# State-space stage of a four-layer kernel: the softplus fix moved next to its subtraction, a wait added on GpSimd, and work re-ordered on TensorE and ScalarE

## The chip, the cores and the metric

The kernel runs on one core of a Trainium2 chip. The metric is the device time of one execution in microseconds; the runs of the kernel before give a median of 2456.47 us. Such a core has TensorE (PE) for matrix products, VectorE (DVE), ScalarE (ACT) and GpSimd (POOL) for elementwise work, and SyncE (SP), which here issues transfers. Each engine works its own list of instructions in order; between engines only semaphores order the work.

## What is computed

The model has four layers over an input of 2 x 2048 tokens of width 256. The change lies in the first, a state-space ("mamba") layer; the mixture of experts, the recurrent feed-forward layer, the attention and the last mixture are untouched. Cut to what matters:

```python
xm, z = jnp.split(x @ W_in.T, 2, axis=-1)               # 512 channels each
xc = silu(causal_conv4(xm) + conv_b)
dt, Bm, Cm = jnp.split(xc @ W_xproj.T, [R, R + N], axis=-1)   # R = 64, N = 16
delta = softplus(dt @ W_dt.T + b_dt)
dA  = exp(delta[..., None] * -exp(A_log))
dBx = delta[..., None] * Bm[:, :, None, :] * xc[..., None]
h = dA_t * h + dBx_t ;  y_t = einsum('ben,bn->be', h, C_t)    # scan over the tokens
out = ((y + D_skip * xc) * silu(z)) @ W_out.T
```

## The kernel before

The state-space stage (`mamba_phase`) works through 8 **units** of 512 tokens; the two batches alternate (`hf` is 0 or 1 in a loop of 4). A unit is 16 **states** n = 0 to 15, one for each component of the state vector, each over all 512 channels, which lie on the 128 partitions in four blocks c = 0 to 3. While a unit's 16 states run, the engines also prepare the next unit (`F`: projections, convolution, gates, dt, softplus) and finish the last one (gating, output projection, residual, norm). The order of all this is written out by hand, state by state.

In a state n each engine does this:

- **GpSimd** makes the products u * B of state n + 2 in two halves q (L399: one instruction of 1024 elements a partition, or in states 13 and 14 two of 512) and behind each half one addition: add (n, 1) and add (n, 3) sum ScalarE's weighted piece into the accumulator (L411). At n = 1 it also computes the scale of the row norm (L374, L376), at n = 13 the new u = delta * xc (L381, twice) and at n = 14 the RMS scale.
- **ScalarE** makes dA for state n + 1 in four pieces (`factor`, L559), weights the token blocks 1 and 3 of the transposed state n - 1 by C (`weighted`, L573; called part (n, 1) and part (n, 3) here, `a_part` in the trace), copies the carry, and does the tasks of `MID_ACT` and `END_ACT`. `END_ACT` stands between the third and the fourth piece of dA. At the end of state 8 that is `silus`: the SiLU of the gates z (L532, 2048 elements a partition) and of xc (L535, L498). `ACT_TABLE_LOAD` is a change of function table, to SiLU, back to exp, to ln, back.
- **VectorE** scans (L787, four pieces), weights and sums the token blocks 0 and 2 (L750), and takes softplus apart in four pairs of operations: `softplus_fix` (L691) and `softplus_sub` (L698) in state 12 and `softplus_add` (L705) in state 13. All of these read two tensors from SBUF, 1024 elements a partition.
- **TensorE** transposes h of state n - 1 in four **turns** j (L929), turns 0 and 1 ahead of the tasks in `EARLY`, turns 2 and 3 ahead of those in `LATE`. There are two PSUM tiles for the turns: turn (n, 1) waits until ScalarE has read part (n - 1, 3), turn (n, 3) until it has read part (n, 1), and turns 0 and 2 wait for VectorE's sums in the same way. Tasks are: f0 and f1 (transposes of the normed rows, which need ScalarE's `hn`), xc0 to xc3 (convolution, in four parts), dt (L871), d0 to d3 (delta), ct, z0 to z3, y0 to y3 (output of the last unit, L847 and L849), o0 and o1 (output projection, L882), g0, g1 and r.

GpSimd's products of state n + 2 wait for turn (n - 1, 3), since the buffer of h is used again, and add (n, j) waits for part (n, j). ScalarE's part (n, j) in turn waits for GpSimd's add (n - 1, j), since the part has one buffer for each j.

```python
EARLY = {2: ["f1"], 3: ["xc0.1"], 4: ["xc0.3"], ... 11: ["d2", "d3"], 12: ["o0"], 13: ["z0"], 14: ["z3"], 15: ["r"]}
LATE = {1: ["y0", "f0"], 2: ["y1", "xc0.0"], 3: ["y2", "xc0.2"], 4: ["y3"], ... 9: ["dt"], 10: ["d0", "d1"], ...}
weighted(U, n, 1, here); factor(U, n + 1, 0, there); ...   # ScalarE, state n
```

## Time and profile before

| | |
|---|---|
| runs, us | 2455.84, 2463.76, 2456.47; median 2456.47 |
| profiled execution | 2460.9 us, span 2459.2 us |
| granted TensorE clock, mean | 0.866 |
| busy over the span | PE 78%, DVE 68%, ACT 48%, POOL 62% |
| the eight units | from 80 to 1125 us of the span |

The profiled execution is 4.4 us above the median. Times below are microseconds from the start of its span. The state-space stage takes a little over two fifths of the span; the other layers follow it behind a barrier, so a microsecond won or lost in a unit is one in the total.

### The profile page before, as it was taken

What the parts mean: (1) busy time and instruction counts of PE and PEld (TensorE: products, weight loads), DVE (VectorE), ACT (ScalarE), POOL (GpSimd) and SP (SyncE); (2) the same over time, 40 slices, a digit from 0 to 9 for tenths busy, and PEclk for the clock granted to TensorE, in tenths of its full rate; (3) what the DMA queues carried; (4) which work ended last, traced back from release to release, by engine and by line L of the source; (5) the groups of instructions that cost most, each with busy time, mean ns of one, the idle gap of its engine ahead of it and who ended that gap; (6) DMA issues with size and microseconds to landing.
All of it is one profiled execution on the core that took longest, in us unless ns stands there. A gap on an engine that the chain in (4) does not pass through costs nothing. (4 is left out here: it accounts for less than half of the span.)

```text
span 2459.2 us, 35798 instructions
## 1 busy us (share of the span) xinstructions
PE 1911.8 (78%) x10252; PEld 1465.2 (60%) x10253; DVE 1678.1 (68%) x3193; ACT 1184.7 (48%) x2021; POOL 1515.8 (62%) x1152
## 2 busy tenths in 40 slices
PE   6787879686979787875599999907877784799970
PEld 2445455554555454544499999904655664699970
DVE  1779898989989898985644444437634897644438
ACT  2677777777777767773232222226632441111112
POOL 1799999999999999994133333335622420355532
PEclk9888979798989888887699999958988896799995
DMA  3111111111101011112411111142000014122226
GB/s 123 38 35 40 39 37 36 39 39 37 39 23 52 27 49 31 43 36 77 165 48 47 47 48 48 41 139 77 9 18 11 9 35 163 42 71 70 70 65 192
DMA packets 76780, 138.63 MB, mean 56 GB/s; under 512 B 10369, under 2 KB 47873, under 8 KB 75858
## 3 DMA queue, kind: packets, MB, share of 16 engines
q1 hardware_dynamic: 62994, 99.67, 12.4%
q0 software_dynamic: 13632, 37.24, 4.8%
q8 instruction: 56, 0.92, 0.2%
q14 instruction: 98, 0.80, 0.1%
HBM read 104.86 MB, written 32.01 MB: 56 GB/s over the span
## 5 line engine op out<-in xcount | busy, mean ns | idle before, releaser
L787 DVE TENSOR_TENSOR_SCAN a_hs<-a_dA,a_carry,a_hs 128x512 f32<-128x512 f32 x512 | 628.3, 1264 | 63.5 <-ACT a_dA L559 53.7
L399 POOL TENSOR_TENSOR a_hs<-a_u,a_b_bc 128x1024 f32<-128x1024 f32 (+1 forms) x292 | 634.9, 2182 | 2.3 <-POOL a_u L381 1.9
L929 PE MATMUL a_h_ps<-k_ident,a_hs 128*128 128x128 f32 x2064 | 328.3, 308 | 174.7 <-DVE a_acc L750 95.6
L929 PEld LDWEIGHTS a_h_ps<-k_ident,a_hs 128*128 128x128 f32 x2064 | 268.4, 158 | 293.5 <-DVE a_hs L787 86.2
L559 ACT ACTIVATE a_dA<-a_delta,a_a_neg 128x512 f32<-128x512 f32 x512 | 350.1, 687 | 39.6 <-DVE a_hs L787 38.4
L411 POOL TENSOR_TENSOR a_acc<-a_acc,a_part 128x512 f32<-128x512 f32 x242 | 331.7, 1371 | 28.6 <-ACT a_part L573 28.3
L573 ACT ACTIVATE a_part<-a_h_ps,a_c_tok 128x512 f32<-128x512 f32 x242 | 166.0, 686 | 203.8 <-PE a_h_ps L929 176.0
L1229 POOL DMA_INDIRECT expert_rows<-m0e_ys,k_pair x71 | 78.7, 1109 | 232.5 <-DVE m0e_ys L1285 221.6
L750 DVE SCALAR_TENSOR_TENSOR a_acc<-a_h_ps,a_c_tok,a_acc 128x512 f32<-128x512 f32 x242 | 176.3, 728 | 46.5 <-PE a_h_ps L929 46.4
L863 PE MATMUL a_fx<-a_hT,a_w_x 128*128 128x512 f32 x432 | 200.9, 597 | 2.2 <-ACT a_halo L495 1.4
L1295 DVE TENSOR_TENSOR m0e_hT<-m0e_gs,m0e_u 128x512 f32<-128x512 f32 x70 | 48.2, 688 | 191.5 <-ACT m0e_gs L1248 191.5
L1248 ACT ACTIVATE m0e_gs<-m0e_g 128x512 f32<-128x512 f32 x71 | 42.4, 597 | 270.0 <-PE m0e_u L1326 270.0
L1252 ACT ACTIVATE m1e_hT<-m1e_u 128x512 f32<-128x512 f32 x71 | 42.4, 597 | 226.3 <-PE m1e_u L1326 226.3
L1326 PE MATMUL m1e_u<-m1e_xT,m1e_wu 128*128 128x128 f32 x1136 | 140.1, 277 | 0.2 <-DVE m1e_wu L1279 0.2
L1326 PE MATMUL m0e_g<-m0e_xT,m0e_wg 128*128 128x128 f32 x1136 | 140.1, 277 | 0.0
L1326 PE MATMUL m0e_u<-m0e_xT,m0e_wu 128*128 128x128 f32 x1136 | 139.5, 276 | 0.0
L1275 DVE TENSOR_SCALAR m1e_xT<-m1e_x,k_ln_w,k_ln_b 128x128 f32<-128x128 f32 x142 | 51.7, 406 | 128.6 <-PE m1e_x L1314 128.6
L1229 POOL DMA_INDIRECT expert_rows<-m1e_ys,k_pair x71 | 70.2, 989 | 104.5 <-DVE m1e_ys L1285 90.1
L1336 PE MATMUL m0e_y<-m0w_down,m0e_hT 128*128 x568 | 134.5, 380 | 0.2 <-DVE m0e_ys L1285 0.2
L1326 PEld LDWEIGHTS m1e_u<-m1e_xT,m1e_wu 128*128 128x128 f32 x1136 | 134.1, 194 | 0.6 <-issue 0.6
L1326 PEld LDWEIGHTS m0e_g<-m0e_xT,m0e_wg 128*128 128x128 f32 x1136 | 134.2, 194 | 0.1
L1336 PE MATMUL m1e_y<-m1w_down,m1e_hT 128*128 x568 | 134.2, 379 | 0.0
(420 smaller groups left out, 3793.2 us busy)
## 6 DMA issues: line engine op xcount, KB each, us to landing
a_b_bc<-b_rows SPq DMA_DIRECT2D x132, 256.0 KB, 3.2
c_y<-expert_rows SPq DMA_DIRECT2D x16, 512.0 KB, 5.6
q_y<-expert_rows SPq DMA_DIRECT2D x16, 512.0 KB, 5.9
norm_rows<-a_x SPq DMA_DIRECT2D x9, 512.0 KB, 3.3
m0w_up<-in_m_up SPq DMA_DIRECT2D x1, 4096.0 KB, 12.1
m0w_gate<-in_m_gate SPq DMA_DIRECT2D x1, 4096.0 KB, 22.2
m0w_down<-in_m_down SPq DMA_DIRECT2D x1, 4096.0 KB, 32.1
c_xl<-in_L_attn_x SPq DMA_DIRECT2D x8, 512.0 KB, 3.7
```

Source lines behind the costliest of these rows:

```text
L399: last = pool.tensor_tensor(hs[k][:, w, :], u[s][:, w, :], b_bc[:, k:k + 1, :].broadcast_to([P, width, T]), ALU.mult)
L411: pool.tensor_tensor(acc[s][:, j, :], acc[s][:, j, :], part[:, j // 2, :], ALU.add).then_inc(s_add, 1)
L559: act.activation(dA[c][:], delta[s][:, c, :], ACT.Exp, scale=a_neg[:, c, k:k + 1]).then_inc(s_da, 1)
L573: act.activation(to, hT_ps[j % 2][:], ACT.Copy, scale=c_tok[s][:, j, k:k + 1]).then_inc(s_part, 1)
L750: dve.scalar_tensor_tensor(out=acc[s][:, j, :], in0=hT_ps[j % 2][:], scalar=weight, in1=acc[s][:, j, :], op0=ALU.mult, op1=ALU.add).then_i ...
L787: dve.tensor_tensor_scan(hs[k][:, c, :], dA[c][:], hs[k][:, c, :], carry[:, hf, c, n:n + 1], ALU.mult, ALU.add).then_inc(s_scan, 1)
L863: last = pe.matmul(ps[:], w_x[:, q, d, k * P:(k + 1) * P], hT[:, d, q:q + T], start=q == 0 and d == 0, stop=q == KC - 1 and d == DC - 1)
L929: last = pe.transpose(hT_ps[j % 2][:, c * P:(c + 1) * P], hs[(n - 1) % NBUF][:, c, j * P:(j + 1) * P], ident[:])
L1229: pool.indirect_dma_start(io["expert_rows"], bass.IndirectOffsetOnAxis(ap=per.pair[:, s:s + 1], axis=0), ys[s % 2][:], None).then_inc(s_st ...
L1275: last = dve.tensor_scalar(xT[k][:, c, :], x_ps[:, c, :], scale[:, c:c + 1], shift[:, c:c + 1], ALU.mult, ALU.add)
L1326: last = pe.matmul(ps[k][:, f, :], w[k][:, c, f * P:(f + 1) * P], xT[k][:, c, :], start=c == 0, stop=c == DC - 1)
L1336: last = pe.matmul(y_ps[k][:], hT[k][:, c, :], w_down[:, c, bass.ds(e * D, D)], start=c == 0, stop=c == FC - 1)
```

## The change

Seven edits, all in `mamba_phase`:

1. `softplus_fix` moves from the middle of state 12 to its end, directly ahead of `softplus_sub` (VectorE).
2. GpSimd, in state 13, waits for both pieces of the subtraction (`s_sub`) ahead of the products of state 15.
3. dt is split: its first two of four matmuls stay at the end of state 9, the other two come behind turn (10, 1) (TensorE).
4. f0 comes ahead of y0 at the end of state 1 (TensorE).
5. The SiLU of z leaves `silus` and becomes `gates`, in state 4 (ScalarE). It is the same z as before, that of the unit in progress, which VectorE multiplies in during the next unit.
6. `softplus_exp` moves behind the second piece of dA in state 11. Part (4, 3) then comes behind the third piece of dA of its state, part (11, 3) behind the fourth (`NEXT_ACT`).
7. In states 8, 10 and 11 (`LONG_END`) the fourth piece of dA comes ahead of the tasks at the end of the state.

```diff
--- before.py
+++ after.py
@@ -234,14 +234,16 @@
         s_p = m.sem("pool_chain")
 
         EARLY = {2: ["f1"], 3: ["xc0.1"], 4: ["xc0.3"], 5: ["xc1.0"], 6: ["xc1.3"], 7: ["xc2.2"], 8: ["xc3.1"],
-                 11: ["d2", "d3"], 12: ["o0"], 13: ["z0"], 14: ["z3"], 15: ["r"]}
-        LATE = {1: ["y0", "f0"], 2: ["y1", "xc0.0"], 3: ["y2", "xc0.2"], 4: ["y3"], 5: ["xc1.1", "xc1.2"], 6: ["xc2.0", "xc2.1"],
-                7: ["xc2.3", "xc3.0"], 8: ["xc3.2", "xc3.3"], 9: ["dt"], 10: ["d0", "d1"], 11: ["ct"], 12: ["o1"], 13: ["z1", "z2"],
+                 10: ["dt.2", "dt.3"], 11: ["d2", "d3"], 12: ["o0"], 13: ["z0"], 14: ["z3"], 15: ["r"]}
+        LATE = {1: ["f0", "y0"], 2: ["y1", "xc0.0"], 3: ["y2", "xc0.2"], 4: ["y3"], 5: ["xc1.1", "xc1.2"], 6: ["xc2.0", "xc2.1"],
+                7: ["xc2.3", "xc3.0"], 8: ["xc3.2", "xc3.3"], 9: ["dt.0", "dt.1"], 10: ["d0", "d1"], 11: ["ct"], 12: ["o1"], 13: ["z1", "z2"],
                 14: ["g0", "g1"]}
-        MID_ACT = {1: ["norms"], 2: ["f1"], 10: ["dt"], 11: ["d2", "d3", "exp"], 13: ["z0"], 14: ["x1", "z2", "z3"]}
+        MID_ACT = {1: ["norms"], 2: ["f1"], 10: ["dt"], 11: ["d2", "d3"], 13: ["z0"], 14: ["x1", "z2", "z3"]}
         END_ACT = {0: ["moments"], 1: ["f0"], 4: ["xc0"], 5: ["own"], 6: ["xc1"], 7: ["xc2"], 8: ["silus"], 10: ["d0", "d1"],
                    11: ["round", "ct"], 12: ["ln"], 13: ["z1"], 14: ["g0", "g1"], 15: ["rows"]}
         LEAD, SHORT = 2, (13, 14)
+        NEXT_ACT = {4: ["gates"], 11: ["exp"]}
+        LONG_END = (8, 10, 11)
         ON_X = ("f0", "f1", "xc0", "xc1", "xc3", "d0", "d2", "ct", "o1", "z1", "z3", "g1")
         FRONT = ["f0", "f1", "xc0", "xc1", "xc2", "xc3", "dt", "d0", "d1", "d2", "d3", "ct", "z0", "z1", "z2", "z3"]
 
@@ -437,6 +439,8 @@
                         pool.wait_ge(s_turn, lin(U, NS * TJ, TJ * (ahead - 2) + TURNED))
                         pool.wait_ge(s_carry, lin(U, NS, ahead - 2 + KEPT))
                         pool.wait_ge(s_bl[ahead % NBUF], loaded(U, ahead))
+                        if n == 13:
+                            pool.wait_ge(s_sub, lin(F, 2, 2))
                         for q in range(2):
                             product(U, ahead, q, hf if ahead < NS else 1 - hf)
                             add(U, n, 2 * q + 1, hf if n else 1 - hf)
@@ -526,10 +530,14 @@
                                           scale=R2[:, bass.ds(tile0 + j, 1)])
                 last.then_inc(s_rows, 1)
 
-            def silus(U, F, s):
+            def gates(U, s):
+
                 for name in ("z2", "z3"):
                     act.wait_ge(s_free[side(name)], count(name, before(U)))
-                act.activation(z[1 - s][:], z[1 - s][:], ACT.Silu).then_inc(s_zc, 1)
+                act.activation(z[s][:], z[s][:], ACT.Silu).then_inc(s_zc, 1)
+
+            def silus(U, F, s):
+
                 for c in range(EC - 1):
                     act.wait_ge(s_free[side(f"xc{c}")], count(f"xc{c}", U))
                     last = act.activation(xc[s][:, c, :], xc[s][:, c, :], ACT.Silu, bias=conv_b[:, c:c + 1])
@@ -624,6 +632,8 @@
                             layer_norms(i * TJ + BT * hf, hf)
                         elif name == "rows":
                             norm_rows(tile0)
+                        elif name == "gates":
+                            gates(U, hf)
                         elif name == "silus":
                             silus(U, F, 1 - hf)
                         else:
@@ -647,13 +657,21 @@
                         for name in MID_ACT.get(n, []):
                             task(name)
                         factor(U, n + 1, 1, there)
-                        weighted(U, n, 3, here)
+                        for name in NEXT_ACT.get(n, []):
+                            task(name)
+                        if n not in NEXT_ACT:
+                            weighted(U, n, 3, here)
                         if n == 15:
                             act.wait_ge(s_rr, lin(U, 1, 1))
                         factor(U, n + 1, 2, there)
+                        if n in LONG_END:
+                            factor(U, n + 1, 3, there)
+                        if n in NEXT_ACT:
+                            weighted(U, n, 3, here)
                         for name in END_ACT.get(n, []):
                             task(name)
-                        factor(U, n + 1, 3, there)
+                        if n not in LONG_END:
+                            factor(U, n + 1, 3, there)
             end = (0, 2 * NB, None)
             for j in OFF:
                 weighted(end, 0, j, 1)
@@ -802,8 +820,6 @@
                         if n == 14:
                             dve.wait_ge(s_free["X"], count("o1", U))
                             rms_stats(tile0, lin(U, 1, 1))
-                        if n == 12:
-                            softplus_fix(F, 1 - hf)
                         if n == 13:
                             softplus_add(F, 1 - hf)
                         scan(2)
@@ -811,6 +827,7 @@
                         summed(U, n, 2, here)
                         summed(U, n, 3, here)
                         if n == 12:
+                            softplus_fix(F, 1 - hf)
                             softplus_sub(F, 1 - hf)
                             dve.wait_ge(s_full["Y"], count("o0", U))
                             dve.wait_ge(s_xn, lin(U, 1, 1))
@@ -867,7 +884,7 @@
                         last = pe.matmul(ps[:], w_z[:, d, k * P:(k + 1) * P], hT[:, d, KC - 1:], start=d == 0, stop=d == DC - 1)
                 elif name == "dt":
                     pe.wait_ge(s_xc, lin(F, 1, 1))
-                    for c in range(EC):
+                    for c in range(EC) if part_ is None else (part_,):
                         last = pe.matmul(ps[0:R + 2 * NS, :], w_proj[:, c, :], xc[s][:, c, :], start=c == 0, stop=c == EC - 1)
                 elif name == "ct":
                     for j in range(TJ):
```

Three places, as the built programs list them. A name's last digit is the number of its buffer.

TensorE at the end of state 1, before: the turns of state 1 (L929, from hs0), y0 (L847, L849), f0 (L859), then the first turn of state 2 (from hs1).

```order
L929 MATMUL a_h_ps0<-k_ident,a_hs0 128x128 x4
L929 MATMUL a_h_ps1<-k_ident,a_hs0 128x128 x4
...
L847 MATMUL a_fy<-a_xc1,a_diag_d 128x512
L849 MATMUL a_fy<-k_ident,a_acc1 128x128 x4
...
L859 MATMUL a_fx<-k_ident,a_hn 128x128 x4
...
L929 MATMUL a_h_ps0<-k_ident,a_hs1 128x128 x4
L929 MATMUL a_h_ps1<-k_ident,a_hs1 128x128 x4
```

And now:

```order
L946 MATMUL a_h_ps0<-k_ident,a_hs0 128x128 x4
L946 MATMUL a_h_ps1<-k_ident,a_hs0 128x128 x4
...
L876 MATMUL a_fx<-k_ident,a_hn 128x128 x4
...
L864 MATMUL a_fy<-a_xc1,a_diag_d 128x512
L866 MATMUL a_fy<-k_ident,a_acc1 128x128 x4
...
L946 MATMUL a_h_ps0<-k_ident,a_hs1 128x128 x4
L946 MATMUL a_h_ps1<-k_ident,a_hs1 128x128 x4
```

f0, which reads `hn`, stands ahead of y0, and the turns of state 2 stand behind both as before.

ScalarE in state 4, before: part (4, 1) (L573), the pieces of dA for state 5 (L559), part (4, 3), the evacuation of xc0.

```order
L573 ACTIVATE a_part<-a_h_ps1,a_c_tok0 128x512
...
L559 ACTIVATE a_dA0<-a_delta0,a_a_neg 128x512
L645 ACTIVATE a_carry<-a_hs3 128x4
L559 ACTIVATE a_dA1<-a_delta0,a_a_neg 128x512
...
L573 ACTIVATE a_part<-a_h_ps1,a_c_tok0 128x512
...
L559 ACTIVATE a_dA2<-a_delta0,a_a_neg 128x512
...
L500 ACTIVATE a_xc1<-a_fx 128x512
L559 ACTIVATE a_dA3<-a_delta0,a_a_neg 128x512
```

And now:

```order
L581 ACTIVATE a_part<-a_h_ps1,a_c_tok0 128x512
...
L567 ACTIVATE a_dA0<-a_delta0,a_a_neg 128x512
L655 ACTIVATE a_carry<-a_hs3 128x4
L567 ACTIVATE a_dA1<-a_delta0,a_a_neg 128x512
...
L537 ACT_TABLE_LOAD
L537 ACTIVATE a_z0<-a_z0 128x2048
...
L567 ACT_TABLE_LOAD
L567 ACTIVATE a_dA2<-a_delta0,a_a_neg 128x512
...
L581 ACTIVATE a_part<-a_h_ps1,a_c_tok0 128x512
...
L504 ACTIVATE a_xc1<-a_fx 128x512
L567 ACTIVATE a_dA3<-a_delta0,a_a_neg 128x512
```

Between the second and the third piece of dA stand two changes of table and the SiLU of z, and part (4, 3) has moved behind the third piece.

VectorE in state 12, before: scans (L787, by piece of dA), sums (L750), the fix (L691), the subtraction (L698).

```order
L787 SCALAR_TENSOR_TENSOR a_hs0<-a_dA0,a_carry,a_hs0 128x512
L787 SCALAR_TENSOR_TENSOR a_hs0<-a_dA1,a_carry,a_hs0 128x512
...
L750 SCALAR_TENSOR_TENSOR a_acc0<-a_h_ps0,a_c_tok0,a_acc0 128x512
...
L691 SCALAR_TENSOR_TENSOR a_acc1<-a_acc1,a_u1 128x1024 x2
...
L787 SCALAR_TENSOR_TENSOR a_hs0<-a_dA2,a_carry,a_hs0 128x512
...
L787 SCALAR_TENSOR_TENSOR a_hs0<-a_dA3,a_carry,a_hs0 128x512
...
L750 SCALAR_TENSOR_TENSOR a_acc0<-a_h_ps0,a_c_tok0,a_acc0 128x512
...
L698 TENSOR_TENSOR a_delta1<-a_delta1,a_acc1 128x1024
```

And now:

```order
L805 SCALAR_TENSOR_TENSOR a_hs0<-a_dA0,a_carry,a_hs0 128x512
L805 SCALAR_TENSOR_TENSOR a_hs0<-a_dA1,a_carry,a_hs0 128x512
...
L768 SCALAR_TENSOR_TENSOR a_acc0<-a_h_ps0,a_c_tok0,a_acc0 128x512
...
L805 SCALAR_TENSOR_TENSOR a_hs0<-a_dA2,a_carry,a_hs0 128x512
...
L805 SCALAR_TENSOR_TENSOR a_hs0<-a_dA3,a_carry,a_hs0 128x512
...
L768 SCALAR_TENSOR_TENSOR a_acc0<-a_h_ps0,a_c_tok0,a_acc0 128x512
...
L709 SCALAR_TENSOR_TENSOR a_acc1<-a_acc1,a_u1 128x1024 x2
...
L716 TENSOR_TENSOR a_delta1<-a_delta1,a_acc1 128x1024
```

All four scans and both sums now stand ahead of the fix.

## Rows read from the trace of the kernel before

**Rows 1.** The page's DMA issues: line, count, size of one, us to landing.
```profile
a_b_bc<-b_rows SPq DMA_DIRECT2D x132, 256.0 KB, 3.2
```

**Rows 2.** Windows, one unit; busy us (instructions) of PE, PEld, DVE, ACT, POOL, then clock.
```profile
457.26:586.76 129.50, 103.77 (x461) 67.39 (x460) 116.36 (x129) 94.93 (x166) 125.71 (x76) 0.87 0.12 38
```

**Rows 3.** Waits of GpSimd in the state-space stage: us in total, times, longest.
```profile
POOL a_acc L411 <- ACT a_part L573: 28.3, 27, 1.7
```

**Rows 4.** Timeline of GpSimd, states 9 to 13: start, length, line; in brackets idle before.
```profile
545.56 1.27 POOL L411 TENSOR_TENSOR a_acc<-a_acc,a_part 128x512 f32<-128x512 f32 x1 [0.61 <-ACT a_part L573]
...
553.68 1.27 POOL L411 TENSOR_TENSOR a_acc<-a_acc,a_part 128x512 f32<-128x512 f32 x1 [1.00 <-ACT a_part L573]
...
562.14 2.50 POOL L399 TENSOR_TENSOR a_hs<-a_u,a_b_bc 128x512 f32<-128x512 f32 x2
...
566.13 1.27 POOL L411 TENSOR_TENSOR a_acc<-a_acc,a_part 128x512 f32<-128x512 f32 x1 [1.50 <-ACT a_part L573]
567.36 3.48 POOL L399 TENSOR_TENSOR a_hs<-a_u,a_b_bc 128x512 f32<-128x512 f32 x2
...
577.70 3.35 POOL L399 TENSOR_TENSOR a_hs<-a_u,a_b_bc 128x1024 f32<-128x1024 f32 x1
```

**Rows 5.** Timeline of VectorE, softplus operations of state 12.
```profile
568.42 3.50 DVE L691 SCALAR_TENSOR_TENSOR a_acc<-a_acc,a_u 128x1024 f32<-128x1024 f32 x2 [1.10 <-ACT a_acc L547]
...
574.86 3.97 DVE L698 TENSOR_TENSOR a_delta<-a_delta,a_acc 128x1024 f32<-128x1024 f32 x2
```

**Rows 6.** Timeline of VectorE, the same operation ahead of the loop.
```profile
68.54 2.36 DVE L691 SCALAR_TENSOR_TENSOR a_acc<-a_acc,a_u 128x1024 f32<-128x1024 f32 x2 [51.15 <-ACT a_acc L547]
```

**Rows 7.** Timeline of TensorE, states 1 and 2.
```profile
487.78 1.63 PE L847 MATMUL a_fy<-a_xc,a_diag_d 128*128 128x512 f32 x2
...
490.55 0.66 PE L859 MATMUL a_fx<-k_ident,a_hn 128*128 128x128 f32 x4 [0.24 <-ACT a_hn L472]
491.05 1.34 PE L929 MATMUL a_h_ps<-k_ident,a_hs 128*128 128x128 f32 x8
```

**Rows 8.** Timeline of GpSimd, the adds (2,1) and (4,3).
```profile
495.24 1.28 POOL L411 TENSOR_TENSOR a_acc<-a_acc,a_part 128x512 f32<-128x512 f32 x1
...
512.96 1.31 POOL L411 TENSOR_TENSOR a_acc<-a_acc,a_part 128x512 f32<-128x512 f32 x1
```

**Rows 9.** Timeline of ScalarE, state 4.
```profile
506.16 0.69 ACT L573 ACTIVATE a_part<-a_h_ps,a_c_tok 128x512 f32<-128x512 f32 x1 [2.46 <-PE a_h_ps L929]
...
508.75 0.69 ACT L573 ACTIVATE a_part<-a_h_ps,a_c_tok 128x512 f32<-128x512 f32 x1 [0.62 <-PE a_h_ps L929]
```

**Rows 10.** Timeline of TensorE, turns (5,0), (5,1) and (8,2), (8,3).
```profile
510.23 1.04 PE L929 MATMUL a_h_ps<-k_ident,a_hs 128*128 128x128 f32 x8
...
533.83 1.04 PE L929 MATMUL a_h_ps<-k_ident,a_hs 128*128 128x128 f32 x8
```

**Rows 11.** Timeline of ScalarE, states 8 to 11.
```profile
536.88 1.28 ACT L532 ACT_TABLE_LOAD   x1
538.18 1.92 ACT L532 ACTIVATE a_z<-a_z 128x2048 f32<-128x2048 f32 x1
540.00 1.93 ACT L535 ACTIVATE a_xc<-a_xc,a_conv_b 128x512 f32<-128x512 f32 x3
...
554.13 0.58 ACT L506 ACTIVATE a_dbc<-a_fy 96x512 f32<-96x512 f32 x1
...
565.27 0.70 ACT L573 ACTIVATE a_part<-a_h_ps,a_c_tok 128x512 f32<-128x512 f32 x1
```

**Rows 12.** Timeline of TensorE, states 9 to 12.
```profile
546.07 5.77 PE L871 MATMUL a_fy<-a_xc,a_w_proj 128*96 128x512 f32 x8
...
566.03 1.11 PE L929 MATMUL a_h_ps<-k_ident,a_hs 128*128 128x128 f32 x4 [3.14 <-ACT a_part L573]
566.94 5.59 PE L882 MATMUL a_fy<-a_w_out,a_z 128*128 128x256 f32 x16
```

**Rows 13.** Windows, columns as in rows 2, at the clock's fall.
```profile
564.00:566.00 2.00, 0.00 (x0) 0.00 (x0) 0.60 (x1) 2.00 (x4) 0.64 (x1) 0.52 0.04 15
```

## The prediction

> **What bounds the kernel now.** I read the page first: 2459.2 us of span, of which the eight units take 1045, and SyncE's loads of B, which take 3.2 us to land [rows 1]. The windows come next. In one unit, from the start of one u product to the next, 129.5 us, GpSimd is busy 125.7, VectorE 116.4, TensorE 103.8 and ScalarE 94.9 [rows 2]. GpSimd is the bound, so the third view is what it waits for: 28.3 us in the whole stage, all for ScalarE's parts [rows 3]. The timeline places them. In the unit shown, add (9, 1) waits 0.61 us, add (10, 1) 1.00 and add (11, 3) 1.50 [rows 4], 3.1 in all, just behind the states in which ScalarE has silus and softplus.
>
> GpSimd's busy time is also longer than its work. The two products of q = 0 in state 12 take 3.48 us [rows 4], against 2.50 of the pair at 562.14, and in the same moment VectorE runs the fix. The fix takes 3.50 us for two operations and the subtraction 3.97 [rows 5]; ahead of the loop, with GpSimd idle, the same pair takes 2.36 [rows 6]. So each of these VectorE operations holds GpSimd up by 0.98 us. GpSimd pays that six times a unit, four times for fix and subtraction.
>
> **The change, part by part.** I follow that unit by its own clock, first what becomes later, then what becomes earlier. What decides is when VectorE has finished the subtraction, X, because GpSimd now waits for it.
>
> *f0 ahead of y0.* Before, y0 ran from 487.78 and was over when f0 started at 490.55, and f0 had waited for `hn` (0.24 us, ScalarE) [rows 7]. y0 filled a gap. Now TensorE stands idle until `hn` comes, does f0, and then y0, while turn (2, 0) is queued behind. Y0's own time is 2.5 us at least (490.31 - 487.78, with the clock rising within it). At the slower clock throughout it is more: it streams as many columns as half of dt's eight passes, which took 5.77 us with a faster end [rows 12], so 2.9 and up to 3.4. I take 3.0, nearest to these. Turn (2, 1) then ends at 491.05 + 1.34 + 3.0 = 495.4, ScalarE's part at 496.1 (0.69 a part, 0.16 for the signal), add (2, 1) starts at 496.25 instead of 495.24 [rows 8]: GpSimd 1.0 late. TensorE stays 3.0 late, since it works without a gap in these states.
>
> *Gates in state 4.* Part (4, 1) was waiting for TensorE [rows 9], so it comes at 506.16 + 3.0 = 509.16. To part (4, 3) it was 2.59 us, 0.62 of it waiting, so 1.97. Now a table change, the SiLU of z and a change back come between: 1.28 + 1.82 + 1.28 and small gaps, 4.5 (the SiLU from 538.18 to 540.00, the change at 536.88 [rows 11]), and one piece of dA, 0.6. Part (4, 3) comes at 516.2 and is there for GpSimd at 517.1; add (4, 3) would want it at 512.96 + 1.0 [rows 8], so 3.1 us more. GpSimd is now 4.1 late. Turn (5, 1), the second half of the row at 510.23 [rows 10], so 510.75, waits for this part and starts at 517.1. TensorE is 6.3 late.
>
> A page of the Trainium skill prices the changes of table higher. "ScalarE: Activation LUTs", section "What ACT_TABLE_LOAD costs", gives about 2.66 us for a switch, load and drain together. By that the gates would cost 7.3 us where I have 4.5. In the trace the load at 536.88 takes 1.28 us and the SiLU starts 0.02 behind it [rows 11]; I go by the trace.
>
> *State 8.* Turn (8, 3) ended at 534.87 [rows 10], now at 541.2. Behind it: part and two pieces of dA 1.8, table 1.3, three SiLUs 1.8 [rows 11], xc3 0.6, part (9, 1) 0.7, table 1.3, two pieces of dA and the carry 1.3, part (9, 3) 0.7. That makes 550.7. The SiLU of z, 1.9, is gone from here, and VectorE gets the fourth piece of dA ahead of it all.
>
> *dt in halves.* Before, all eight passes stood in one piece at 546.07 and took 5.77 us at the slower clock, with turns (10, 0) and (10, 1) behind [rows 12]. Now half of it fills the time before part (9, 3), and the other half, about 1.7 at full clock, follows turn (10, 1): dt is evacuated at about 553.3 instead of 554.13 [rows 11]. The waits of add (9, 1) and add (10, 1) go, 1.6 us. From there ScalarE is busy without a gap to part (11, 3), at 565.27 before. Its list is the same but for the two pieces of dA that have come ahead of it: 565.27 - 0.8 + 1.2 = 565.7. GpSimd, 4.1 late less 1.6, wants add (11, 3) at 564.6 + 2.5 = 567.1: this wait goes too, 1.5 us.
>
> *End of state 12.* TensorE's o0 waits for turn (12, 1), and that for part (11, 3). Turn (12, 1) came after 3.14 us of idleness, and o0 took 5.59 us, to 572.5 [rows 12], as the granted clock had fallen to 0.52 in 564 to 566 [rows 13]. I see no less idleness after the change, so o0 ends 0.4 later, at 572.9. Turn (12, 2) 0.5 and VectorE's sum 0.7 follow, then fix and subtraction, four operations, 4.7 uncontended [rows 6]. Add (12, 3) needs turn (12, 3), which o0 has delayed as well, so it falls between them and holds VectorE up once more, 1.2. X = 572.9 + 0.5 + 0.7 + 4.7 + 1.2 = 580.0. Before, fix ran while o0 ran; that cover is gone.
>
> *The sum.* Before, the products of state 15 started at 577.70 [rows 4] and lost another 0.98 to the subtraction, as good as 578.7. Now they start at 580.0: 1.3 us later. From there to the next unit all is as before (u and one add still meet softplus_add). Of GpSimd's own account: 4.1 us of new waits, 3.1 old ones gone, 3.9 of held-up operations mostly gone, and 4 or so of the new wait in their place. Eight units: 8 x 1.3 = 10 us. Against the profiled 2460.9 that is 2471; against the median 2456.5, 4.4 lower, it is **2466.5**.
>
> Bounds: y0 at 2.5 or 3.4 gives -0.5 to +0.4 a unit; o0 at full clock, half its time at most, up to -2.8; no add between the four operations -1.2; the clock falling in state 5, below, +2. Costed at nothing: SyncE's loads of B, which come two states ahead of use; without that cover each of the 16 in a unit could show up to its 3.2 us [rows 1]. The edit in state 10 only changes places within ScalarE's full stretch.
>
> **Rivals.**
>
> (A) *Faster: TensorE's delays are absorbed.* If `hn` is there early or the parts are not needed so soon, X comes 3.0 earlier, at 577.0, 1.7 better than before: 8 x 1.7 = 14 less, 2443. If both delays vanish, X is 573.7, 5 better a unit, 2416. For it: the removed waits and hold-ups are real, 7 us a unit. Against: y0 before f0 plainly filled a gap. It decides at part (11, 3): 1.3 us earlier than I say, and the sign turns.
>
> (B) *No change.* X falls within 0.9 us of the old start. GpSimd then swaps hold-ups for a wait of like length. 2456.
>
> (C) *Slower still: TensorE's clock falls in state 5.* Turn (5, 0) would be followed by about 3.3 us of idleness; 3.14 us of it was followed by the slower clock in state 12. The convolution parts behind it would run slower for some 3 to 5 us, TensorE loses about 2 more, and these states have no gap to win it back: 8 x 3.3 = 26, 2483.
>
> (D) *A change of table holds ScalarE longer than its row.* If each of the two new changes cost its own 1.28 us once more, part (4, 3) and X would come 2.6 later: 8 x 3.9 = 31, 2488. Against it: in rows 11 the SiLU starts right behind its load. The page named above would have it so, at about this size.
>
> **How the numbers follow.** Chances: my case 0.42, A 0.31, B 0.15, C 0.11, D 0.01. My own case spans +3 to +18 us. A measurement of this kernel tells 0.3%, 7.4 us, from no change; a fifth of my case, 0.09, lies within that. Faster 0.31 (A); same 0.15 + 0.09 = 0.24; slower 0.33 + 0.11 + 0.01 = 0.45. The range leaves out the better part of A's second half and D: 2436 to 2486.
>
> **What would show it.** In the profile after: the wait of GpSimd for VectorE's subtraction once a unit, 3 to 4 us; new waits of about 1 us at add (2, 1) and 3 us at add (4, 3); none at (9, 1), (10, 1) and (11, 3); TensorE idle for 2.6 us ahead of f0 and 3.3 us ahead of turn (5, 1); fix and subtraction together 5 to 6 us instead of 7.5; 16 more table loads; a unit of 130.8 us. The prediction is wrong if part (4, 3) comes in time, or if fix starts before o0 is through, or if the unit is shorter than 129.

## The result and the profile after

The changed kernel takes 2475.7 us (median of 5 runs, 2474.28 to 2476.69), the kernel before 2456.47 (5 runs): a ratio of 1.0067, 95% interval 1.0055 to 1.0079. It is slower, as forecast. The medians are 19 us apart, the ratio stands for 16.5 us (13.5 to 19.4), and 10 were forecast; in the later groups the kernel before has medians of 2458.1 to 2458.7, against which it is 17 us. The profiled execution has a span of 2475.0 us against 2459.2, 15.8 more; the other 3 us of the 19 come from the two profiled executions, which were 4.4 us above the median of before and 1.0 above that of the changed kernel.

I cut each unit at two rows of GpSimd that no work of another engine holds up: P1, the power of the layer norm in state 1 (L374 before, L376 after), and the end of the u products. The first unit's u products start at 201.80 after the change and the last unit's at 1121.69, seven units of 131.41 between them; before, 197.27 and 1105.66, 129.77 each. From the end of u to P1 it is 23.4 us in every unit of every kernel here. All the difference lies between P1 and the end of the next u. Here are the eight stretches in order, from GpSimd's timeline (start of P1 to start plus length of u):

| unit | 1 | 2 | 3 | 4 | 5 | 6 | 7 | 8 | sum |
|---|---|---|---|---|---|---|---|---|---|
| before | 106.41 | 106.37 | 106.80 | 106.06 | 106.66 | 106.00 | 106.56 | 105.99 | 850.85 |
| after | 108.73 | 107.02 | 108.90 | 107.08 | 108.93 | 107.06 | 108.95 | 107.12 | 863.79 |

So there are two kinds of unit, in turn. The short ones lost 0.97 us on average (3.86 in four), the long ones 2.27 (9.08 in four), 12.94 together. Another 2.2 us stand ahead of the first unit's P1 (98.70 against 96.50), and 0.7 behind the last; the first of these has no visible relation to the time: over the profiled executions here the first P1 lies between 95.2 and 99.2, and it is 99.12 in e3_both_back, which is faster than before. The prediction worked out unit 4, a short one.

GpSimd's waits in the stage, for [rows 3]:

```profile
POOL a_acc L413 <- ACT a_part L581: 39.9, 28, 2.4
POOL a_hs L401 <- DVE a_delta L716: 32.0, 8, 4.6
```

And its timeline, first in a long unit (unit 3), then in the short unit 4 that answers to [rows 4, 8]:

```profile
361.26 1.66 POOL L376 TENSOR_TENSOR a_pw<-a_pv,a_halfneg 128x8 f32<-128x8 f32 x1
...
372.58 1.28 POOL L413 TENSOR_TENSOR a_acc<-a_acc,a_part 128x512 f32<-128x512 f32 x1 [2.38 <-ACT a_part L581]
...
392.58 1.27 POOL L413 TENSOR_TENSOR a_acc<-a_acc,a_part 128x512 f32<-128x512 f32 x1 [2.21 <-ACT a_part L581]
...
443.38 1.28 POOL L413 TENSOR_TENSOR a_acc<-a_acc,a_part 128x512 f32<-128x512 f32 x1 [0.85 <-ACT a_part L581]
...
456.43 2.35 POOL L401 TENSOR_TENSOR a_hs<-a_u,a_b_bc 128x1024 f32<-128x1024 f32 x1 [3.44 <-DVE a_delta L716]
...
493.61 1.66 POOL L376 TENSOR_TENSOR a_pw<-a_pv,a_halfneg 128x8 f32<-128x8 f32 x1
...
503.65 1.27 POOL L413 TENSOR_TENSOR a_acc<-a_acc,a_part 128x512 f32<-128x512 f32 x1 [1.09 <-ACT a_part L581]
...
523.64 1.27 POOL L413 TENSOR_TENSOR a_acc<-a_acc,a_part 128x512 f32<-128x512 f32 x1 [2.20 <-ACT a_part L581]
...
586.77 2.35 POOL L401 TENSOR_TENSOR a_hs<-a_u,a_b_bc 128x1024 f32<-128x1024 f32 x1 [4.57 <-DVE a_delta L716]
...
593.79 2.27 POOL L413 TENSOR_TENSOR a_acc<-a_acc,a_part 128x512 f32<-128x512 f32 x1 [1.08 <-ACT a_part L581]
...
596.02 4.67 POOL L383 TENSOR_TENSOR a_u<-a_delta,a_xc 128x1024 f32<-128x1024 f32 x2
```

In both units add (2, 1) and add (4, 3) wait, and the products of state 15 wait for the subtraction; add (9, 1) and (10, 1) no longer do, and add (11, 3) waits only in the long unit (0.85). X is P1 + 93.16 in the short unit and P1 + 95.17 in the long one. Their difference, 2.0, is 1.29 at add (2, 1), and the rest arises at part (11, 3). TensorE shows where it comes from. First f0, y0 and turns (2, 0) and (2, 1) in the long unit, then the same in the short one; then turn (5, 1) and the convolution part behind it, long and short:

```profile
365.50 1.12 PE L876 MATMUL a_fx<-k_ident,a_hn 128*128 128x128 f32 x4 [0.71 <-ACT a_hn L476]
366.41 1.92 PE L864 MATMUL a_fy<-a_xc,a_diag_d 128*128 128x512 f32 x2
368.11 1.92 PE L866 MATMUL a_fy<-k_ident,a_acc 128*128 128x128 f32 x8
369.82 1.88 PE L946 MATMUL a_h_ps<-k_ident,a_hs 128*128 128x128 f32 x8
...
497.83 1.12 PE L876 MATMUL a_fx<-k_ident,a_hn 128*128 128x128 f32 x4 [2.56 <-ACT a_hn L476]
498.74 1.92 PE L864 MATMUL a_fy<-a_xc,a_diag_d 128*128 128x512 f32 x2
500.45 1.44 PE L866 MATMUL a_fy<-k_ident,a_acc 128*128 128x128 f32 x8
501.72 1.04 PE L946 MATMUL a_h_ps<-k_ident,a_hs 128*128 128x128 f32 x8
...
392.48 1.11 PE L946 MATMUL a_h_ps<-k_ident,a_hs 128*128 128x128 f32 x4 [3.19 <-ACT a_part L581]
393.38 2.90 PE L880 MATMUL a_fx<-a_hT,a_w_x 128*128 128x512 f32 x4
...
523.54 0.65 PE L946 MATMUL a_h_ps<-k_ident,a_hs 128*128 128x128 f32 x4 [2.81 <-ACT a_part L581]
524.03 1.98 PE L880 MATMUL a_fx<-a_hT,a_w_x 128*128 128x512 f32 x4
```

The granted clock of these stretches, in windows of 2 us (columns as in rows 2, the clock third from the end): it is 0.50 until y0 is through in the long unit and rises within y0 in the short one, and behind turn (5, 0) it falls in the long unit alone.

```profile
368.00:370.00 2.00, 2.00 (x10) 1.88 (x9) 0.13 (x1) 0.40 (x1) 2.00 (x1) 0.50 0.28 96
...
500.00:502.00 2.00, 2.00 (x12) 1.55 (x11) 0.00 (x0) 0.73 (x2) 2.00 (x2) 0.69 0.16 63
...
394.00:396.00 2.00, 2.00 (x4) 0.82 (x3) 0.81 (x1) 1.68 (x4) 2.00 (x1) 0.64 0.00 0
...
524.00:526.00 2.00, 2.00 (x8) 0.97 (x7) 1.92 (x2) 2.00 (x5) 2.00 (x2) 1.00 0.01 3
```

The idleness before turn (5, 1) is 3.19 us where the clock had fallen and 2.81 where it had not. y0 and turns (2, 0) and (2, 1) take 5.3 us in the long unit (366.41 to 369.82 + 1.88) and 4.0 in the short one; turn (5, 1) and its convolution part 3.8 against 2.5. Each of the two costs the long unit 1.3.

ScalarE, state 4 and part (11, 3), and VectorE's fix and subtraction, all in the short unit, for [rows 5, 9, 11]. (VectorE's softplus is three pairs of operations, fix, subtraction and addition, not four as said ahead of the prediction.)

```profile
515.67 0.69 ACT L581 ACTIVATE a_part<-a_h_ps,a_c_tok 128x512 f32<-128x512 f32 x1 [2.26 <-POOL a_acc L413]
...
517.67 1.28 ACT L537 ACT_TABLE_LOAD   x1
518.97 1.91 ACT L537 ACTIVATE a_z<-a_z 128x2048 f32<-128x2048 f32 x1
520.89 1.28 ACT L567 ACT_TABLE_LOAD   x1
...
522.82 0.67 ACT L581 ACTIVATE a_part<-a_h_ps,a_c_tok 128x512 f32<-128x512 f32 x1
...
572.24 0.70 ACT L581 ACTIVATE a_part<-a_h_ps,a_c_tok 128x512 f32<-128x512 f32 x1
```

```profile
579.87 4.55 DVE L709 SCALAR_TENSOR_TENSOR a_acc<-a_acc,a_u 128x1024 f32<-128x1024 f32 x2
584.35 2.35 DVE L716 TENSOR_TENSOR a_delta<-a_delta,a_acc 128x1024 f32<-128x1024 f32 x2
```

### The profile page after: what moved, and what is told of

It is laid out like the page before. It is cut to its first block and busy times, and to the rows that moved or that the text cites. A ratio compares the mean times of both kernels' runs of the same rounds, so it can differ in the third digit from the quotient of the medians.

```text
span 2475.0 us, 35814 instructions
## 1 busy us (share of the span) xinstructions
PE 1915.2 (77%) x10252; PEld 1469.5 (59%) x10253; DVE 1671.1 (68%) x3193; ACT 1205.8 (49%) x2037; POOL 1483.4 (60%) x1152
## 5 line engine op out<-in xcount | busy, mean ns | idle before, releaser
L401 POOL TENSOR_TENSOR a_hs<-a_u,a_b_bc 128x1024 f32<-128x1024 f32 (+1 forms) x292 | 618.3, 2125 | 34.3 <-DVE a_delta L716 32.0
L413 POOL TENSOR_TENSOR a_acc<-a_acc,a_part 128x512 f32<-128x512 f32 x242 | 319.5, 1321 | 40.2 <-ACT a_part L581 39.9
L880 PE MATMUL a_fx<-a_hT,a_w_x 128*128 128x512 f32 x432 | 206.4, 610 | 2.2 <-ACT a_halo L499 1.4
```

Source lines behind the costliest of these rows:

```text
L401: last = pool.tensor_tensor(hs[k][:, w, :], u[s][:, w, :], b_bc[:, k:k + 1, :].broadcast_to([P, width, T]), ALU.mult)
L413: pool.tensor_tensor(acc[s][:, j, :], acc[s][:, j, :], part[:, j // 2, :], ALU.add).then_inc(s_add, 1)
L880: last = pe.matmul(ps[:], w_x[:, q, d, k * P:(k + 1) * P], hT[:, d, q:q + T], start=q == 0 and d == 0, stop=q == KC - 1 and d == DC - 1)
```

## The experiments

Twelve kernels, five rounds each, in three groups; each group had its own runs of before beside it (medians 2458.06, 2458.66 and 2458.59 us). "Unit" is the mean of seven in the profiled execution, from start to start of the u products; from end to end it is 131.28 in the changed kernel and differs by 0.01 at most in the others. A number in the text below is a median in us, then the ratio to before with its interval.

| run | us | ratio | unit |
|---|---|---|---|
| after | 2475.7 | 1.0067 | 131.41 |
| e1_y0_first | 2459.76 | 1.0010 | 129.55 |
| e2_gates_in_8 | 2462.25 | 1.0019 | 129.85 |
| e3_both_back | 2449.25 | 0.9966 | 128.75 |
| e4_fix_mid | 2483.16 | 1.0103 | 132.89 |
| e5_e3_fix_mid | 2447.09 | 0.9950 | 127.88 |
| e6_e3_no_wait | 2459.78 | 1.0002 | 129.22 |
| e7_e3_fix_mid_no_wait | 2443.18 | 0.9936 | 128.06 |
| e8_e3_dt_whole | 2457.62 | 1.0001 | 129.03 |
| e9_residual_first | 2475.04 | 1.0065 | 131.30 |
| e10_e7_residual_first | 2444.69 | 0.9945 | 128.06 |
| e12_e5_residual_first | 2444.72 | 0.9941 | 127.81 |
| e11_before_dt_halves | 2447.58 | 0.9954 | 127.98 |

**y0 and gates undone, one by one and together.** The theory was that these two moves are the loss and the rest of the change is a gain.

```diff
-        LATE = {1: ["f0", "y0"], ...
+        LATE = {1: ["y0", "f0"], ...
```

> The changed kernel with one edit undone: y0 ahead of f0 again at the end of state 1. Theory (TensorE and ScalarE set the end of the subtraction): TensorE stands 2.56 us idle ahead of f0 in the changed kernel and its turns come 2.2 us late; without that the wait of add (2,1), 1.1 to 2.4 us, goes, and the subtraction ends some 2.2 us earlier: 8 x 2.2 = 18 us less than the changed kernel, about 2458. Rival (GpSimd's new wait for the subtraction soaks up whatever is won ahead of it, and the order of f0 and y0 is of no account): 2475, with the wait for the subtraction 2 us longer.

```diff
-        END_ACT = {... 8: ["silus"], ...
+        END_ACT = {... 8: ["gates", "silus"], ...
-        NEXT_ACT = {4: ["gates"], 11: ["exp"]}
+        NEXT_ACT = {11: ["exp"]}
```

> The changed kernel with one edit undone: the SiLU of z back in state 8, ahead of those of xc, behind the fourth piece of dA. Theory: the wait of add (4,3), 2.2 us, and TensorE's idle time of 2.81 us ahead of turn (5,1) go, but the SiLU's 1.9 us come back on ScalarE's path in state 8: about 1 us a unit won, 2467. Rival (the second pair of table loads and the early SiLU are the whole loss): 2456 or less.

> Both undone: y0 ahead of f0, and the SiLU of z back in state 8. What is left of the change: fix next to the subtraction, GpSimd's wait, dt in halves, exp and the fourth pieces of dA earlier. Theory: the two add up, 3.2 us a unit: about 2450, below the kernel before, since the removed waits of adds (9,1), (10,1) and (11,3) then count. Rival (the wait for the subtraction itself costs what the change loses): 2465 or more, still slower than before.

Measured: y0 back 2459.76, 1.0010 (1.0001 to 1.0019), so y0's place costs 16 us; gates back 2462.25, 1.0019 (1.0010 to 1.0027), 13 us, more than expected; both back 2449.25, 0.9966 (0.9953 to 0.9979), 26 us, faster than before. (By the ratios these are 14, 12 and 25.) With both back no add of states 2 to 8 waits any more, and X is P1 + 90.13 in the best unit (575.30 - 485.17) and up to P1 + 92.68 in others, always behind a wait of 3.43 for the subtraction:

```profile
575.30 2.36 POOL L401 TENSOR_TENSOR a_hs<-a_u,a_b_bc 128x1024 f32<-128x1024 f32 x1 [3.43 <-DVE a_delta L716]
```

**The fix ahead of the scans, in the changed kernel.** Here my theory was that the fix at the end of state 12 is late without need.

```diff
+                        if n == 12:
+                            softplus_fix(F, 1 - hf)
                         if n == 13:
                             softplus_add(F, 1 - hf)
...
                         if n == 12:
-                            softplus_fix(F, 1 - hf)
                             softplus_sub(F, 1 - hf)
```

> The changed kernel with one edit undone: the fix back in the middle of state 12, beside o0; GpSimd still waits for the subtraction. Theory: fix then fills the 4.92 us in which VectorE waits for the turn behind o0, the subtraction ends about 3 us earlier, and GpSimd's two hold-ups of 0.98 us by the fix are paid out of its wait of 4.57: 8 x 3 = 24 us less than the changed kernel, 2452. Rival (the end of state 12 is bound by something else, such as the turns or ln): no change, 2475.

Measured 2483.16, 1.0103 (1.0087 to 1.0118): slower still, a clear miss. GpSimd's wait for the subtraction did shrink to 1.16 us in seven units, yet X is P1 + 96.04 in unit 4. There five adds wait between P1 and X, where the short unit above has two. On TensorE the clock falls behind turn (5, 0) in seven of the eight units, not in every second, and the convolution part takes 3.62 us (2.8 in units 1 and 3) instead of 1.98:

```profile
523.47 1.11 PE L947 MATMUL a_h_ps<-k_ident,a_hs 128*128 128x128 f32 x4 [2.86 <-ACT a_part L581]
524.38 3.62 PE L881 MATMUL a_fx<-a_hT,a_w_x 128*128 128x512 f32 x4
```

This unit sits in the same place as the short one above, and its idleness before the turn is nearly the same (2.86 and 2.81). With the slower part behind it, the next turn, (5, 2), starts at P1 + 35.2, as in the long units of the changed kernel (34.9) and not as in its short ones (32.2). The exception is unit 2, which is the longest of all (110.22). There no clock falls; the fix itself is held up, for 9.62 us, while GpSimd's instructions beside it keep their usual length, and GpSimd then waits 7.58 us for the subtraction:

```profile
309.32 9.62 DVE L709 SCALAR_TENSOR_TENSOR a_acc<-a_acc,a_u 128x1024 f32<-128x1024 f32 x2 [3.50 <-ACT a_acc L555]
...
324.30 2.35 POOL L401 TENSOR_TENSOR a_hs<-a_u,a_b_bc 128x1024 f32<-128x1024 f32 x1 [7.58 <-DVE a_delta L716]
```

Where the gates are in state 8 (before, e2, e3 and those built on e3, e11) the convolution part takes 1.88 us in every unit: no fall. Where they are in state 4 the clock falls in some units or in all. It falls in all eight of e1_y0_first as well (idleness of 3.04 to 3.20 us, the part 2.80 to 3.60), and that kernel is 16 us faster than the changed one: there turn (5, 2) still starts at P1 + 31.3 to 32.8. So it is how late TensorE is behind the fall that goes with a long unit, not the fall alone. If this is what e4 lost by, the placing of the fix is harmless once y0 and the gates are back. This is e3_both_back with the edit of e4_fix_mid:

```diff
+                        if n == 12:
+                            softplus_fix(F, 1 - hf)
...
-                            softplus_fix(F, 1 - hf)
                             softplus_sub(F, 1 - hf)
```

> Both harmful moves undone (y0 first, gates in state 8), and the softplus fix back ahead of the scans of halves 2 and 3 of state 12; GpSimd's wait for the subtraction stays. In e4 the fix in this place made the kernel slower, and TensorE's clock fell in state 5 of every unit, which does not show when y0 and the gates stand where they were. Theory (e4 lost by that clock fall, the fix itself comes earlier): the subtraction ends about 1 us earlier behind part (11,3), so 8 x 1 less than e3_both_back, 2441. Rival (the fix ahead holds the scans behind the wait for ScalarE's round, and its two operations meet GpSimd's products again, 2 x 0.98 a unit): 2449 or more, up to 2457.

Measured 2447.09, 0.9950 (0.9932 to 0.9969). It is the sign of the theory without its size: the interval overlaps that of e3_both_back. In the trace X is P1 + 90.2 and P1 + 91.4 in turn, where e3_both_back has 90.1 to 92.7, and no clock falls in state 5. So the fix in this place is not slow by itself; it cost e4 its 7.5 us in a kernel that also has y0 behind f0 and the gates in state 4. Which of these two it takes is not isolated.

**GpSimd's wait.** Both from e3_both_back; the second has the fix ahead of the scans as well.

```diff
-                        if n == 13:
-                            pool.wait_ge(s_sub, lin(F, 2, 2))
```

> e3_both_back without GpSimd's wait for the subtraction; fix and subtraction stay together at the end of state 12 and run beside GpSimd's products of state 15. Theory (the wait of 3.43 us a unit only takes the place of four hold-ups of 0.98 us, 3.9): the time stays within 6 us of 2449. Rival (the wait is a cost of its own, GpSimd could have used the time): 8 x 2.5 less, about 2430. Third (the subtraction, contended, comes later, and softplus_add and TensorE behind it with it): 8 x 1.5 more, 2461.

> The fix back ahead of the scans, no wait of GpSimd, y0 first, gates in state 8: what is left of the change is dt in halves, softplus's exp and the fourth pieces of dA ahead of a part. Theory (these edits removed the waits of add (9,1), (10,1) and (11,3), 3.1 us a unit, and part (11,3) is what the end of state 12 hangs on): faster than before, by 8 x 1 to 8 x 3, 2434 to 2450. Rival (the gain of e3_both_back came from the wait and the moved fix alone): 2456 as before.

With the fix at the end, taking the wait away costs 10 us: 2459.78, 1.0002 (0.9991 to 1.0013), the third case. Fix and subtraction of e6, then TensorE's z0 behind the addition of o0, and last the two adds of GpSimd that wait for what follows:

```profile
566.04 3.46 DVE L707 SCALAR_TENSOR_TENSOR a_acc<-a_acc,a_u 128x1024 f32<-128x1024 f32 x2
569.43 4.52 DVE L714 TENSOR_TENSOR a_delta<-a_delta,a_acc 128x1024 f32<-128x1024 f32 x2
```

```profile
574.59 3.78 PE L882 MATMUL a_fy<-a_hT,a_w_z 128*128 128x512 f32 x4 [4.49 <-DVE k_hidden L734]
```

In e3_both_back the same z0:

```profile
575.87 3.64 PE L884 MATMUL a_fy<-a_hT,a_w_z 128*128 128x512 f32 x4 [2.74 <-DVE k_hidden L736]
```

The two adds of GpSimd in e6:

```profile
574.22 1.27 POOL L413 TENSOR_TENSOR a_acc<-a_acc,a_part 128x512 f32<-128x512 f32 x1 [2.49 <-ACT a_part L579]
...
581.04 1.27 POOL L413 TENSOR_TENSOR a_acc<-a_acc,a_part 128x512 f32<-128x512 f32 x1 [3.25 <-ACT a_part L579]
```

The pair takes 8.0 us beside GpSimd's products and 6.2 with GpSimd waiting (3.87 and 2.35 in e3_both_back). It stands in VectorE's queue ahead of the addition of o0 and the scans of state 13, so all of that is late and TensorE is idle for 4.49 us ahead of z0 instead of 2.74; z0 runs at the slower clock in both. The 3.43 us of wait are replaced by 5.7 of other waits. With the fix ahead of the scans it is otherwise: 2443.18, 0.9936 (0.9920 to 0.9951), against 0.9966 (0.9953 to 0.9979) with both the wait and the fix at the end. With the subtraction alone and contended, GpSimd's adds of state 13 wait 0.47 us at most. So the change's pair "fix at the end, GpSimd waits" costs some 6 us (the two intervals just miss each other; the eight stretches from P1 to the end of u, added up, say 5.6), and its two halves belong together only because the first makes the second needed.

**dt in halves.** Once taken away from e3_both_back, as shown, and once put alone into the kernel before (there with the line that lets dt be issued in parts).

```diff
-                 10: ["dt.2", "dt.3"], 11: ["d2", "d3"], ...
+                 11: ["d2", "d3"], ...
-                7: ["xc2.3", "xc3.0"], 8: ["xc3.2", "xc3.3"], 9: ["dt.0", "dt.1"], ...
+                7: ["xc2.3", "xc3.0"], 8: ["xc3.2", "xc3.3"], 9: ["dt"], ...
```

> e3_both_back with dt in one piece behind turn (9, 3), as before the change. Theory (dt whole stands ahead of turns (10,0) and (10,1), so add (10,1) waits 1.0 us again and part (11,3) comes about 1 later): 8 x 1 more, 2457. Rival (ScalarE's full stretch sets part (11,3) anyway, the halves bring nothing): 2449.

> The kernel before the change with dt in halves as the only edit: y0 first, gates in state 8, fix ahead of the scans, no wait, ScalarE's list as before. Theory (dt in one piece at the slower clock kept turns (10,0) and (10,1) waiting, and the wait of add (10,1), 1.0 us, and part of that of (11,3) go with the halves): 8 x 1 less, 2448. Rival (the gain of e7 is that of the exp and of the fourth pieces of dA, which have moved on ScalarE): 2456 as before. Third (both are needed: ScalarE's full stretch takes over): 2453.

Taken away: 2457.62, 1.0001 (0.9988 to 1.0014), 8 us. Alone in the kernel before: 2447.58, 0.9954 (0.9941 to 0.9967), 11 us faster, as expected. GpSimd's waits for parts fall from the 28.3 us of [rows 3] to 13.4:

```profile
POOL a_acc L411 <- ACT a_part L573: 13.4, 18, 1.8
```

Its P1 to the end of u is 103.6 and 105.6 in turn, against 106.0 and 106.6 before. The halves are the part of the change that works. What e7 has over e11, exp and the fourth pieces of dA ahead of a part, is not told apart from nothing (0.9936 against 0.9954, the intervals overlap). One caution: the profiled execution of e3_both_back is 3.2 us above its median and those of e6 and e8 are 3.4 and 3.9 below theirs, so the units of the table (128.75, 129.22, 129.03) differ by far less than the medians; the verdicts on e6 and e8 rest on the runs.

**The addition of o0 first.** After reading the trace I took the wait of add (13, 3), 1.08 us, for the term that the prediction lacked: TensorE idle for 3.41 us ahead of z0, behind the subtraction, then at the slower clock:

```profile
587.34 3.78 PE L884 MATMUL a_fy<-a_hT,a_w_z 128*128 128x512 f32 x4 [3.41 <-DVE k_hidden L736]
```

These three runs move VectorE's addition of o0 ahead.

```diff
                         if n == 12:
+                            dve.wait_ge(s_full["Y"], count("o0", U))
+                            dve.wait_ge(s_xn, lin(U, 1, 1))
+                            residual(0, fy, tile0).then_inc(s_free["Y"], 1)
                             softplus_fix(F, 1 - hf)
                             softplus_sub(F, 1 - hf)
-                            dve.wait_ge(s_full["Y"], count("o0", U))
-                            dve.wait_ge(s_xn, lin(U, 1, 1))
-                            residual(0, fy, tile0).then_inc(s_free["Y"], 1)
```

> The kernel after the change, with one edit: VectorE adds o0's result to the hidden state ahead of fix and subtraction, not behind them. Theory (the part of the slowdown that the prediction lacked is TensorE's idleness of 3.4 us ahead of z0 behind the subtraction, the fall of its clock and the wait of add (13,3)): z0 follows turn (12,3) without a gap and at full clock, the wait for the subtraction is 0.7 longer (one more operation of 0.67 ahead of it), and state 13 and the u products behind it come about 1.0 earlier: a unit 0.3 to 0.6 shorter, 2471 to 2473. Rival (idleness of TensorE there costs nothing): a unit 0.7 longer, 2481.

> e7 (fix ahead of the scans, no wait of GpSimd, y0 first, gates in state 8) with the addition of o0's result ahead of the subtraction. TensorE's idleness ahead of z0 there was 1.54 us and one of 1.03 ahead of turn (13,0), at full clock, and no add of state 13 waited. Theory: nothing of GpSimd's hangs on it, 2443 as e7, within 4. Rival (softplus_add comes 0.7 later with the subtraction): 8 x 0.7 more, 2449.

> e5 (fix ahead of the scans, with GpSimd's wait) with the addition of o0's result ahead of the subtraction. In e5 TensorE was idle for 2.18 us ahead of z0 and add (13,3) waited 0.30 us. Theory: the subtraction ends 0.7 later, add (13,3) no longer waits: 0.4 a unit longer, 2450. Rival (the fall of TensorE's clock in z0 costs more than that): 2443 or less.

The first fell as a theory. It measured 2475.04, 1.0065 (1.0053 to 1.0077), no change. The idleness ahead of z0 and the wait of add (13, 3) are gone, as meant (z0 first, then GpSimd), and nothing is won:

```profile
585.13 1.88 PE L884 MATMUL a_fy<-a_hT,a_w_z 128*128 128x512 f32 x4
...
588.06 2.35 POOL L401 TENSOR_TENSOR a_hs<-a_u,a_b_bc 128x1024 f32<-128x1024 f32 x1 [4.57 <-DVE a_delta L716]
590.42 1.27 POOL L413 TENSOR_TENSOR a_acc<-a_acc,a_part 128x512 f32<-128x512 f32 x1
591.65 3.33 POOL L401 TENSOR_TENSOR a_hs<-a_u,a_b_bc 128x1024 f32<-128x1024 f32 x1
594.95 2.24 POOL L413 TENSOR_TENSOR a_acc<-a_acc,a_part 128x512 f32<-128x512 f32 x1
597.15 4.66 POOL L383 TENSOR_TENSOR a_u<-a_delta,a_xc 128x1024 f32<-128x1024 f32 x2
```

softplus_add costs GpSimd about 0.98 us twice in these kernels, wherever it falls. Here it meets a product (3.33) and an add (2.24); in the changed kernel's short unit it meets the add and the wait of 1.08 stands in place of the second; in long units it meets the add and u (5.64 instead of 4.66). From X to the end of u that makes 13.75 us here, 13.92 and 13.73 in the changed kernel, 13.75 in e3_both_back. I had measured to the start of u, where half of it is left out. The other two say the same: 2444.69, 0.9945 (0.9930 to 0.9960), as e7; and 2444.72, 0.9941 (0.9927 to 0.9955), where 2450 was expected and neither that nor a gain over e5 shows.

## Why the prediction was right, and where its size was off

- **Sign and place: right.** The new waits are at add (2, 1) and (4, 3) and before state 15; those at (9, 1) and (10, 1) went. y0's place and the gates' cost 16 and 13 us by experiment, and no other part of the change costs as much.
- **f0 ahead of y0: right in the short units, too small in the long.** Forecast: TensorE idle for 2.6 and 3.0 late, add (2, 1) 1.0 late; measured 2.56 idle and a wait of 1.09. In long units y0 runs wholly at the slower clock, the bound of 3.4 that I kept for the range, and so does turn (2, 0), which I had not counted: the wait is 2.38.
- **Gates in state 4: right mechanism, the wait 0.9 us too long.** Forecast 3.1 of wait and 3.3 of TensorE's idleness; measured 2.20 and 2.81. The gates themselves were priced right: from part (4, 1) to part (4, 3) 7.07 forecast, 7.15 measured (515.67 to 522.82). What was too dear is "TensorE stays 3.0 late": part (4, 1) starts at P1 + 22.06, where 22.83 was forecast, and by then it waits for GpSimd's add (2.26 us) and no longer for TensorE. Rival D is refuted: the SiLU starts 0.02 us behind the load, and the second load right at its end. By the Trainium skill's "ScalarE: Activation LUTs", "What ACT_TABLE_LOAD costs", a switch would have taken 2.66 us; the trace here shows 1.28.
- **State 10 and part (11, 3).** Forecast 0.4 later counted from P1, measured 0.3 earlier in the short unit (78.63 against 78.94), 2.3 later in the long one (81.26).
- **X.** Forecast P1 + 93.7 (580.0 - 486.33), measured P1 + 93.16 in the same unit. Inside it two errors partly cancel, so that it came so near is luck: the fix started 1.5 earlier than forecast (part (11, 3) came 0.7 earlier, and o0 took 4.83 us and not 5.59), and fix and subtraction took 6.8 us instead of 5.9. The fix was held up by 2.2 us (4.55 against 2.36), not by 1.2. The wait of GpSimd was forecast 3 to 4 and is 3.44 or 4.57.
- **"From there to the next unit all is as before": right,** 13.7 to 14.0 us from X to the end of u in all kernels that have the wait, and e9 shows that what looks like a loss there is none.
- **The step that was off is the factor of eight.** 8 x 1.3 took one unit for all. That unit measured 1.02 (107.08 - 106.06), but four of eight are of the other kind, with 2.3. Rival C was in those: the clock falls behind turn (5, 0), at 1.3 us where I had priced 2. It is not an alternative to my case but takes turns with it. Rival B, no change, is nearer than its chance suggests: in the short units X is 0.8 later than the old start as the sum counts it (P1 + 92.37), within B's 0.9, yet each of them is 0.65 to 1.13 us longer. The sum for the units is 12.94 where 10 was forecast; the rest of the 19 us between the medians is 2.2 ahead of the first unit, 0.7 behind the last, and the profiled executions' distances from their medians. The forecast gave its own case +3 to +18 us; 16.5 by the ratio and 19 by the medians are at its upper end.
- **Rival A's price was wrong.** It said 2416 if both delays vanish. e3_both_back is the nearest kernel to that, at 2449 (its SiLU of z is also back on ScalarE in state 8, 1.9 us). TensorE's 6.3 us were never GpSimd's in full: with both back, three parts of states 5 to 8 in unit 4 wait for GpSimd's adds (0.66, 0.85 and 1.05 us on ScalarE), so TensorE's time runs into GpSimd's own, and X came 3.0 earlier than in the changed kernel (90.13 against 93.16), not 6.

What stays open: why the clock falls in every second unit of the changed kernel and in seven units of e4_fix_mid, at an idleness of nearly the same length (2.81 without a fall, 2.80 to 3.21 with one). Units alternate in most kernels here, before included, but not in e2, e3, e4, e6 and e8. Something carried over from the unit before may enter, or a difference between the two batches, whose units the loop writes out one after the other; the second alone does not force it, since units 3 to 8 of e2 are all alike (106.3 to 106.5). No run isolates either.

## What to carry to other kernels

When a loop's iterations are not all alike, price the edit in each kind before multiplying: here the kind that I read lost 1.0 us and the other 2.3. Test a bundle by parts, because one good part (dt in halves, 11 us alone) can be buried by others (y0's place and the gates', 26 us together). And measure between rows that nothing holds up: up to the start of an operation, a hold-up that has only changed places looks like a loss.

## What the runs showed of the hardware that I had not expected

- The granted clock of TensorE is a term of the schedule, not a background. The same four instructions of a convolution part took 1.98 us, 2.90 or 3.62 (at a clock of 1.00, rising within it, and at 0.50), behind idleness of 2.81, 3.19 and 2.86 us. A fall alone does not decide: e1_y0_first has one in each unit and is 16 us faster than the changed kernel, which has one in every second unit.
- A two-operand operation of VectorE on 128x1024 costs GpSimd up to 0.98 us: on a product (2.35 to 3.33), an add (1.27 to 2.24) or u (4.66 to 5.64). It can also be VectorE alone that pays. A pair that takes 2.36 alone took 3.4 to 5.5 in most places; 4.55 in the changed kernel's short unit, where GpSimd's add (12, 3) kept its 1.30; and 9.62 in unit 2 of e4_fix_mid, beside four groups of GpSimd rows of unchanged length. What decides who waits is not shown here.
- Letting GpSimd wait instead can pay, by 10 us in e3_both_back against e6, where a long queue stands behind the pair on VectorE.
